# Context attentions: TensorE's transposes issued one by one behind products, with VectorE's and ScalarE's order of a couple of units to match

## Chip, cores and metric

The kernel runs on one core of a Trainium2 chip. The metric is the device time of one execution in microseconds; before the change the median of three runs is 2290.49 us (2285.55 to 2293.77). The time reported for a run is taken around the whole program, and the profile's span lies inside it.

## What is computed

The reference is a stack of four layers on x of shape (8, 64, 256) or, flattened, 512 rows of 256. Each layer adds a cross attention to a context of 1601 keys, a self attention and a feed-forward part, all in float32. Three of the four cross attentions (layer 0's second one, layer 2's, layer 3's) have 16 heads and go through the function that the change touches. Cut to what matters, for layer 2:

```python
scores = jnp.einsum('bhnd,bhmd->bhnm', qh, kh) * scale      # 8 batches, 16 heads, 64 queries, 1601 keys
attn = jax.nn.softmax(scores, axis=-1)
out = jnp.einsum('bhnm,bhmd->bhnd', attn, vh)
```

The kernel does not project the context to keys and values. It takes each head's query through the key weights first, so that the scores are a product of a 128-wide query with the raw 128-wide context, and it takes the weighted sum of the raw context through the value weights afterwards, in another function (`late_values`).

## The kernel before, in words

`cross_attention` (L830) is called three times, at L1860 and L2079 (the latter function twice). A **unit** is two heads of one batch: 2 x 64 = 128 query rows on 128 partitions. There are 64 units (8 batches, 8 units each). Two units make a **couple**, 32 couples in an attention. A step of the engines' loops is 16 units, the first step is written out ahead of the loop.

A float32 operand is kept as two parts of type float32r, a high and a low one, and each product is made of three TensorE products into the same PSUM columns (`three_passes`, L635 to L639): high x high (L637), high x low (L638), low x high (L639).

For each unit v this is done:

- **Scores** (`scores`, L915): four column groups of 290, 512, 512 and 288 keys, three products each, so 12 products, into PSUM banks 0 to 3. The first two groups (802 columns) are the first half, with the semaphore `scores_half`, the others (799) the second, with `scores_ready`.
- **Maximum** (`maximum`, L1079): VectorE takes the maximum of each half (L1082, L1084) and makes the negative scaled maximum `ntop` of both (L1087).
- **Exponents** (`exponents`, L1019): ScalarE writes the exponentials of each half to `probs` (two buffers, called slots: slot 0 is named `normed` in the profile and holds the couple's first unit, slot 1 is named `probs` and holds the second); a small read instruction behind each half fetches the row sums.
- **Transposes** (`turn`, L933): the 1601 probabilities are 13 chunks of 128 keys (the last one has 65). TensorE transposes each chunk (L937) into one of PSUM banks 4, 5 and 7. The chunks form four groups, 4 + 4 + 4 + 1, one bank for a group at a time (`turned_bank`), so a group's first transpose waits until VectorE has emptied that bank (`low_kept`).
- **High and low part** of the transposed probabilities: ScalarE copies a group as high part `pTh` (`keep`, L1031, L1037), then VectorE writes the rest as low part `pTl` (`low`, L1090, L1095), which frees the bank and lets the value products begin.
- **Values** (`values`, L956): both units of a couple at once: 13 chunks, three products of 256 columns each, 39 products, all into PSUM bank 6. VectorE then writes the result back to `q` (`store`, L1100, L1106 or L1108).

The order on each engine is written out by hand. TensorE's order for a couple starting with unit v (`body`, L971) is: transposes of group 0 of the previous couple's second unit; scores(v); transposes of groups 1 and 2 of that second unit; value products of group 0 of the previous couple; transpose of group 3; value products of group 1; scores(v+1); transposes of groups 0 and 1 of unit v; value products of group 2; transposes of group 2; value products of group 3; transpose of group 3 of unit v. So there are five runs of transposes, of 4, 8, 1, 8 and 4, with the last 1 ahead of the next couple's 4. ScalarE's order (L1042): copies of groups 0, 1 and 2 of the previous second unit, both halves of the exponents of v, copy of group 3, in two couples of four a copy of the next batch's keys as high part (`high`, L1014), copies of groups 0 and 1 of v, both halves of the exponents of v+1, copies of groups 2 and 3. VectorE's order (L1110): low part 0 of the previous second unit, maximum of v, low parts 1, 2 and 3, maximum of v+1, low parts 0 and 1 of v, store, low parts 2 and 3 of v. GpSimd (L874) splits the queries of the couple after next and the next keys into parts, and the sync engine (L861) fetches the keys of the next batches; the change touches neither.

These lines of waits matter for the order:

```python
pe.wait_ge(low_kept, 4 * (2 * c + 1) + g + 1)   # in values: low part g of the couple's second unit
act.wait_ge(value_ready if g == 3 else value_part, c if g == 3 else 3 * (c - 1) + g + 1)   # in keep, first unit
```

The first lets a group's value products begin only when VectorE has written that group's low part for the couple's second unit. The second lets a copy of the first unit overwrite `pTh` only when the previous couple's value products of that group are done.

## Time and profile before

| | before |
|---|---|
| median of three runs | 2290.49 us (2285.55 to 2293.77) |
| the profiled execution | 2297.82 us, span 2296.0 us |
| mean granted TensorE clock | 0.93 |
| TensorE products busy | 2042.5 us, 89% |
| TensorE weight loads busy | 1749.3 us, 76% |
| VectorE busy | 1379.2 us, 60% |
| ScalarE busy | 1124.4 us, 49% |
| GpSimd busy | 512.6 us, 22% |
| DMA, mean over the span | 63 GB/s |

The three attentions lie at about 203 to 597, 1107 to 1497 and 1714 to 2107 us of the span. The profile names lines of the kernel and the tiles by the program's names: `ps<-cTh,qh` is a score product, `ps<-pTh,ch` a value product, `ps<-ident,normed` and `ps<-ident,probs` transposes of slots 0 and 1. PE is TensorE's products, PEld its weight loads, which are records of their own; DVE is VectorE, ACT is ScalarE. In a timeline each row gives the start, the duration, the engine, line and operation, shapes and a count of merged instructions. A product's duration contains its way through the array, so products that follow one another overlap in the records: what one costs is read from one start to the next.

### The profile page before, as it was taken

What the parts mean: (1) busy time and instruction counts of PE and PEld (TensorE: products, weight loads), DVE (VectorE), ACT (ScalarE), POOL (GpSimd) and SP (SyncE); (2) the same over time, 40 slices, a digit from 0 to 9 for tenths busy, and PEclk for the clock granted to TensorE, in tenths of its full rate; (3) what the DMA queues carried; (4) which work ended last, traced back from release to release, by engine and by line L of the source; (5) the groups of instructions that cost most, each with busy time, mean ns of one, the idle gap of its engine ahead of it and who ended that gap; (6) DMA issues with size and microseconds to landing.
All of it is one profiled execution on the core that took longest, in us unless ns stands there. A gap on an engine that the chain in (4) does not pass through costs nothing. (4 is left out here: it accounts for less than half of the span.)

```text
span 2296.0 us, 41893 instructions
## 1 busy us (share of the span) xinstructions
PE 2042.5 (89%) x14948; PEld 1749.3 (76%) x14948; DVE 1379.2 (60%) x2704; ACT 1124.4 (49%) x2256; POOL 512.6 (22%) x412
## 2 busy tenths in 40 slices
PE   4776999999886998489899999987979999999898
PEld 1654999999655885277699999956859999997577
DVE  6463777777445443831677777724447777776366
ACT  2243666666423432321566666613436666664254
POOL 2323222221011330200322222002332222220034
PEclk9687999999987998789999999977999999999799
DMA  5153010010041213432100100001221001000022
GB/s 211 25 233 128 31 45 31 29 44 0 26 156 57 79 53 136 188 139 83 45 30 31 45 29 29 0 13 66 78 83 45 31 30 44 29 15 0 19 78 76
DMA packets 32314, 144.01 MB, mean 63 GB/s; under 512 B 3632, under 2 KB 9136, under 8 KB 28848
## 3 DMA queue, kind: packets, MB, share of 16 engines
q1 hardware_dynamic: 32176, 142.23, 17.2%
q8 instruction: 80, 1.31, 0.2%
q14 instruction: 58, 0.48, 0.1%
HBM read 125.59 MB, written 13.90 MB: 61 GB/s over the span
## 5 line engine op out<-in xcount | busy, mean ns | idle before, releaser
L1037 ACT ACTIVATE pTh<-ps 128x512 fp32r<-128x512 f32 (+1 forms) x768 | 353.9, 519 | 382.5 <-PE ps L937 380.4
L1095 DVE TENSOR_TENSOR pTl<-ps,pTh 128x512 fp32r<-128x512 f32 (+1 forms) x768 | 415.7, 582 | 129.0 <-ACT pTh L1037 128.8
L637 PE MATMUL ps<-pTh,ch 128*128 128x256 f32 (+1 forms) x1248 | 383.5, 307 | 2.3 <-DVE pTl L1095 2.2
L638 PE MATMUL ps<-pTl,ch 128*128 128x256 f32 (+1 forms) x1248 | 348.4, 279 | 0.0
L639 PE MATMUL ps<-pTh,cl 128*128 128x256 f32 (+1 forms) x1248 | 348.0, 279 | 0.0
L637 PE MATMUL ps<-cTh,qh 128*128 128x512 f32 (+2 forms) x768 | 276.9, 361 | 15.2 <-POOL ql L891 8.0
L639 PE MATMUL ps<-cTh,ql 128*128 128x512 f32 (+2 forms) x768 | 269.6, 351 | 0.0
L638 PE MATMUL ps<-cTl,qh 128*128 128x512 f32 (+2 forms) x768 | 268.8, 350 | 0.0
L1082 DVE TENSOR_REDUCE top<-ps 128x1 f32<-128x802 f32 x192 | 189.2, 986 | 110.7 <-PE ps L639 110.7
L637 PEld LDWEIGHTS ps<-pTh,ch 128*128 128x128 f32 (+1 forms) x1248 | 235.1, 188 | 15.8 <-DVE pTl L1095 12.1
L638 PEld LDWEIGHTS ps<-pTl,ch 128*128 128x128 f32 (+1 forms) x1248 | 235.7, 189 | 0.0
L639 PEld LDWEIGHTS ps<-pTh,cl 128*128 128x128 f32 (+1 forms) x1248 | 234.5, 188 | 0.0
L1084 DVE TENSOR_REDUCE top<-ps 128x1 f32<-128x799 f32 x192 | 188.7, 983 | 14.8 <-PE ps L639 4.6
L1026 ACT ACTIVATE normed<-ps,ntop 128x802 f32<-128x802 f32 x192 | 176.9, 927 | 32.6 <-DVE ntop L1087 30.5
L937 PE MATMUL ps<-ident,probs 128*128 128x128 f32 (+1 forms) x1248 | 182.9, 272 | 3.5 <-DVE pTl L1095 2.4
L937 PE MATMUL ps<-ident,normed 128*128 128x128 f32 (+1 forms) x1248 | 183.4, 273 | 1.7 <-DVE pTl L1095 1.7
L1026 ACT ACTIVATE probs<-ps,ntop 128x802 f32<-128x802 f32 x192 | 177.0, 938 | 0.0
L637 PEld LDWEIGHTS ps<-cTh,qh 128*128 128x128 f32 x768 | 146.7, 191 | 36.0 <-POOL ql L891 10.5
L638 PEld LDWEIGHTS ps<-cTl,qh 128*128 128x128 f32 x768 | 147.7, 192 | 17.4
L639 PEld LDWEIGHTS ps<-cTh,ql 128*128 128x128 f32 x768 | 147.0, 191 | 16.9
L937 PEld LDWEIGHTS ps<-ident,probs 128*128 128x128 f32 (+1 forms) x1248 | 146.9, 140 | 5.5 <-ACT probs L1026 3.1
L937 PEld LDWEIGHTS ps<-ident,normed 128*128 128x128 f32 (+1 forms) x1248 | 147.0, 141 | 2.4 <-DVE pTl L1095 2.4
(351 smaller groups left out, 3585.9 us busy)
## 6 DMA issues: line engine op xcount, KB each, us to landing
w<-l1f_w_in SPq DMA_DIRECT2D x16, 1024.0 KB, 8.0
raw<-ctxT_in SPq DMA_DIRECT2D x16, 801.0 KB, 4.3
raw<-ctx_in SPq DMA_DIRECT2D x14, 832.0 KB, 4.4
wg<-l0f_guide_in SPq DMA_DIRECT2D x10, 704.0 KB, 5.1
z<-ctx_in SPq DMA_DIRECT2D x8, 832.0 KB, 12.9
z<-z SPq DMA_DIRECT2D x8, 832.0 KB, 10.6
keys<-ctx_in SPq DMA_DIRECT2D x8, 832.0 KB, 11.2
zT<-zT SPq DMA_DIRECT2D x8, 801.0 KB, 14.0
```

What stands on the lines that cost most here:

```text
L637: pe.matmul(out, high, moving_high, start=start, stop=False)
L638: pe.matmul(out, high, moving_low, start=False, stop=False)
L639: return pe.matmul(out, low, moving_high, start=False, stop=stop)
L937: last = pe.transpose(ps[0:w, turned_bank[slot][g], k * P:(k + 1) * P], probs[slot][:, chunk * P:chunk * P + w], ident[:])
L1026: nc.scalar.activation(probs[slot][:, cols], flat[:, cols], ACT.Exp, bias=ntop[:, slot:slot + 1], scale=scale, accum_out=sums[:, bass.ds(2 ...
L1037: nc.scalar.activation(pTh[0:w, PARTS[g][0]:PARTS[g][0] + n, slot, :], ps[0:w, turned_bank[slot][g], 0:n * P].rearrange("p (k r) -> p k r" ...
L1082: dve.tensor_reduce(top[:, slot, 0:1], flat[:, half_cols[0]], AX.X, ALU.max).then_inc(top_step, 1)
L1084: dve.tensor_reduce(top[:, slot, 1:2], flat[:, half_cols[1]], AX.X, ALU.max)\
L1095: dve.tensor_tensor(pTl[0:w, at, slot, :], ps[0:w, turned_bank[slot][g], 0:n * P].rearrange("p (k r) -> p k r", r=P), pTh[0:w, at, slot, : ...
```

## The change

Each transpose is issued by itself behind one product. The functions `scores` and `values` get a parameter `beside`, a function that is called behind each of their products with its number; `turn` issues one transpose. In a couple, the products of scores(v) are numbered 0 to 11, and one transpose of the previous second unit follows each of the products 1 to 4 (group 0) and 8 to 11 (group 1). The value products are numbered 0 to 38: behind 0, 2, 4 and 6 stand group 2's transposes, behind 8 the one of group 3. The value products of chunks 0 to 4 (15 of them) come next, then scores(v+1) without transposes, and then chunks 5 to 12, with the transposes of unit v behind products 15 to 18 (group 0), 19 to 22 (group 1), 25, 27, 29 and 31 (group 2) and 36 (group 3). The wait for `probs_half` ahead of scores(v) stays inside `scores` alone.

On ScalarE the copy of group 2 of the previous second unit moves from ahead of unit v's exponents to behind them, and the second half of unit v+1's exponents moves from ahead of the copies of groups 2 and 3 to behind them. On VectorE the first half's maximum of unit v moves ahead of low part 0 of the previous second unit.

The number of products, transposes, copies and maxima stays the same. The diff, cut to its core:

```diff
 
     @block.tensor
     def _(pe):
-        def scores(u, step, first):
+        def scores(u, step, first, beside):
...
+            k, at = (u // 2) % 2, slice((u % 2) * P, (u % 2) * P + P)
             for n in range(4):
                 if n in (0, 2) and not (first and u == 0):
                     pe.wait_ge(probs_ready if n else probs_half, v)
-                last = three_passes(pe, flat[:, score_cols[n]], qh[:, k, at:at + P],
-                                    ql[:, k, at:at + P], cTh[:, i, score_cols[n]],
-                                    cTl[:, i, score_cols[n]], True, True)
+                cols = score_cols[n]
+                pe.matmul(flat[:, cols], qh[:, k, at], cTh[:, i, cols], start=True, stop=False)
+                beside(3 * n)
+                pe.matmul(flat[:, cols], qh[:, k, at], cTl[:, i, cols], start=False, stop=False)
+                beside(3 * n + 1)
+                last = pe.matmul(flat[:, cols], ql[:, k, at], cTh[:, i, cols], start=False, stop=True)
                 if n == 1:
                     last.then_inc(scores_half, 1)
-            last.then_inc(scores_ready, 1)
...
+                if n == 3:
+                    last.then_inc(scores_ready, 1)
+                beside(3 * n + 2)
+
+        def turn(g, k, v, slot, first=False):
+
+            if k == 0 and slot:
+                pe.wait_ge(low_kept, 4 * v + (-2, -1, 0, 1)[g])
+            if k == 0 and not slot and g != 2 and (g == 3 or not first):
+                pe.wait_ge(low_kept, 4 * v + (-1, 0, None, 1)[g])
+            chunk = PARTS[g][k]
+            w = keys_in(chunk)
+            last = pe.transpose(ps[0:w, turned_bank[slot][g], k * P:(k + 1) * P],
+                                probs[slot][:, chunk * P:chunk * P + w], ident[:])
+            if chunk == PARTS[g][-1]:
+                last.then_inc(turned_ready, 1)
+
...
-            pe.wait_ge(low_kept, 4 * (2 * c + 1) + g + 1)
-            for chunk in PARTS[g]:
-                w = keys_in(chunk)
-                moving = [t[0:w, chunk].rearrange("p u r -> p (u r)") for t in (pTh, pTl)]
-                at = slice(chunk * CD, chunk * CD + CD)
-                last = three_passes(pe, value_psum, ch[0:w, i, at], cl[0:w, i, at],
-                                    moving[0], moving[1], chunk == 0, chunk == KCH - 1)
-            last.then_inc(value_ready if g == 3 else value_part, 1)
+            if chunk % 4 == 0:
+                pe.wait_ge(low_kept, 4 * (2 * c + 1) + g + 1)
+            w = keys_in(chunk)
+            th, tl = (t[0:w, chunk].rearrange("p u r -> p (u r)") for t in (pTh, pTl))
+            at = slice(chunk * CD, chunk * CD + CD)
+            pe.matmul(value_psum, ch[0:w, i, at], th, start=chunk == 0, stop=False)
+            if beside is not None:
+                beside(3 * chunk)
+            pe.matmul(value_psum, ch[0:w, i, at], tl, start=False, stop=False)
+            if beside is not None:
+                beside(3 * chunk + 1)
+            last = pe.matmul(value_psum, cl[0:w, i, at], th, start=False, stop=chunk == KCH - 1)
+            if chunk == PARTS[g][-1]:
+                last.then_inc(value_ready if g == 3 else value_part, 1)
+            if beside is not None:
+                beside(3 * chunk + 2)
+
+        def alone(n):
+            pass
...
                 if first and u == 0:
-                    scores(u, step, first)
-                    scores(u + 1, step, first)
+                    scores(u, step, first, alone)
+                    scores(u + 1, step, first, alone)
                     for g in range(4):
-                        turn_first(g, v, True)
+                        for k in range(len(PARTS[g])):
+                            turn(g, k, v, 0, True)
                     continue
-                pe.wait_ge(probs_half, v)
-                turn_second(0, v - 1)
-                scores(u, step, first)
-                turn_second(1, v - 1)
-                turn_second(2, v - 1)
-                values(0, c - 1, i, first and u == 2, new_batch)
-                turn_second(3, v - 1)
-                values(1, c - 1, i)
-                scores(u + 1, step, first)
-                turn_first(0, v)
-                turn_first(1, v)
-                values(2, c - 1, i)
-                turn_first(2, v)
-                values(3, c - 1, i)
-                turn_first(3, v)
+
+                def second_with_scores(n):
+                    if 1 <= n < 5:
+                        turn(0, n - 1, v - 1, 1)
+                    elif n >= 8:
+                        turn(1, n - 8, v - 1, 1)
+
+                def second_with_values(n):
+                    if n < 8 and n % 2 == 0:
+                        turn(2, n // 2, v - 1, 1)
+                    elif n == 8:
+                        turn(3, 0, v - 1, 1)
+
+                def first_with_values(n):
+                    if 15 <= n < 19:
+                        turn(0, n - 15, v, 0)
+                    elif 19 <= n < 23:
+                        turn(1, n - 19, v, 0)
+                    elif 25 <= n < 33 and n % 2:
+                        turn(2, (n - 25) // 2, v, 0)
+                    elif n == 36:
+                        turn(3, 0, v, 0)
+
+                scores(u, step, first, second_with_scores)
+                values(0, c - 1, i, second_with_values, first and u == 2, new_batch)
+                for chunk in range(1, 4):
+                    values(chunk, c - 1, i, second_with_values)
...
-        values(0, c, 1)
-        values(1, c, 1)
-        values(2, c, 1)
-        values(3, c, 1)
+            for k in range(len(PARTS[g])):
+                turn(g, k, last, 1)
+        for chunk in range(KCH):
+            values(chunk, c, 1)
 
     @block.scalar
     def _(act):
@@ -1048,12 +1070,11 @@
                 before = not (first and u == 0)
                 if before:
                     keep(0, v - 1, 1)
-                if before:
                     keep(1, v - 1, 1)
-                    keep(2, v - 1, 1)
                 exponents(v, 0, first and u < 2, 0)
                 exponents(v, 0, first and u < 2, 1)
                 if before:
+                    keep(2, v - 1, 1)
                     keep(3, v - 1, 1)
                 if at == 0 and not (final and i):
                     high(n, cTh[:, 1 - i])
@@ -1062,9 +1083,9 @@
                 keep(0, v, 0, c if before else None)
                 keep(1, v, 0, c if before else None)
                 exponents(v + 1, 1, first and u < 2, 0)
-                exponents(v + 1, 1, first and u < 2, 1)
                 keep(2, v, 0, c if before else None)
                 keep(3, v, 0, c if before else None)
+                exponents(v + 1, 1, first and u < 2, 1)
 
         body(0, True)
         with act.Fori(1, STEPS - 1) as step:
@@ -1076,10 +1097,13 @@
 
     @block.vector
     def _(dve):
-        def maximum(v, slot):
+        def maximum_of_half(v, slot):
 
             dve.wait_ge(scores_half, v + 1)
             dve.tensor_reduce(top[:, slot, 0:1], flat[:, half_cols[0]], AX.X, ALU.max).then_inc(top_step, 1)
+
+        def maximum(v, slot):
+
             dve.wait_ge(scores_ready, v + 1)
             dve.tensor_reduce(top[:, slot, 1:2], flat[:, half_cols[1]], AX.X, ALU.max)\
                 .then_inc(top_step, 1)
@@ -1113,6 +1137,7 @@
                 v = step * UNITS + u
                 c = step * COUPLES + u // 2
                 before = not (first and u == 0)
+                maximum_of_half(v, 0)
                 if before:
                     low(0, v - 1, 1)
                 maximum(v, 0)
@@ -1120,6 +1145,7 @@
                     low(1, v - 1, 1)
                     low(2, v - 1, 1)
                     low(3, v - 1, 1)
+                maximum_of_half(v + 1, 1)
                 maximum(v + 1, 1)
                 low(0, v, 0)
                 low(1, v, 0)
```

## Rows read from the trace of the kernel before

**Rows 1.** Windows, all engines, inside an attention: busy us, instructions, clock, DMA share, GB/s.
```profile
core 0: us, PE busy (x) PEld busy (x) DVE busy (x) ACT busy (x) POOL busy (x), PEclk, DMA share, GB/s
300.00:350.00 50.00, 50.00 (x370) 47.07 (x369) 36.80 (x64) 33.24 (x71) 11.21 (x10) 1.00 0.11 35
```

**Rows 2.** TensorE's timeline: start, duration; first products of couples 1 and 31, second attention.
```profile
1118.02 0.38 PE L637 MATMUL ps<-cTh,qh 128*128 128x290 f32 x1
...
1478.54 0.38 PE L637 MATMUL ps<-cTh,qh 128*128 128x290 f32 x1
```

**Rows 3.** TensorE's timeline inside one couple of the first attention.
```profile
302.07 0.39 PE L639 MATMUL ps<-cTh,ql 128*128 128x512 f32 x1
302.30 0.30 PE L637 MATMUL ps<-cTh,qh 128*128 128x288 f32 x1
...
302.56 0.30 PE L639 MATMUL ps<-cTh,ql 128*128 128x288 f32 x1
302.70 1.03 PE L937 MATMUL ps<-ident,probs 128*128 128x128 f32 x8
...
303.70 0.28 PE L638 MATMUL ps<-pTl,ch 128*128 128x256 f32 x1
...
304.98 0.27 PE L937 MATMUL ps<-ident,probs 128*65 128x128 f32 x1
...
305.34 0.28 PE L638 MATMUL ps<-pTl,ch 128*128 128x256 f32 x1
...
307.50 0.40 PE L639 MATMUL ps<-cTh,ql 128*128 128x512 f32 x1
```

**Rows 4.** TensorE's weight loads (PEld) in the same stretch, timeline.
```profile
302.07 0.19 PEld L637 LDWEIGHTS ps<-cTh,qh 128*128 128x128 f32 x1
302.30 0.19 PEld L638 LDWEIGHTS ps<-cTl,qh 128*128 128x128 f32 x1
...
303.46 0.19 PEld L637 LDWEIGHTS ps<-pTh,ch 128*128 128x128 f32 x1
303.57 0.19 PEld L638 LDWEIGHTS ps<-pTl,ch 128*128 128x128 f32 x1
...
305.11 0.19 PEld L637 LDWEIGHTS ps<-pTh,ch 128*128 128x128 f32 x1
```

**Rows 5.** VectorE's timeline beside that couple.
```profile
302.34 0.98 DVE L1082 TENSOR_REDUCE top<-ps 128x1 f32<-128x802 f32 x1
303.24 0.97 DVE L1084 TENSOR_REDUCE top<-ps 128x1 f32<-128x799 f32 x1
304.25 0.21 DVE L1087 TENSOR_SCALAR ntop<-top 128x1 f32<-128x1 f32 x1
304.38 1.28 DVE L1095 TENSOR_TENSOR pTl<-ps,pTh 128x512 fp32r<-128x512 f32 x2
...
307.93 0.99 DVE L1082 TENSOR_REDUCE top<-ps 128x1 f32<-128x802 f32 x1 [0.94 <-PE ps L639]
```

**Rows 6.** Groups by line and shape, 240 to 560 us: count, busy us, mean ns.
```profile
L1095 DVE TENSOR_TENSOR pTl<-ps,pTh 128x512 fp32r<-128x512 f32 x160 | 104.8, 683 | 8.6 <-ACT pTh L1037 8.4
```

**Rows 7.** ScalarE's timeline beside that couple.
```profile
303.33 1.09 ACT L1037 ACTIVATE pTh<-ps 128x512 fp32r<-128x512 f32 x2 [1.80 <-PE ps L937]
304.59 0.93 ACT L1026 ACTIVATE normed<-ps,ntop 128x802 f32<-128x802 f32 x1 [0.17 <-DVE ntop L1087]
305.42 0.19 ACT L1026 ACTIVATION_READ_ACCUMULATOR normed<-ps,ntop  x1
...
306.41 0.26 ACT L1037 ACTIVATE pTh<-ps 65x128 fp32r<-65x128 f32 x1
306.57 1.54 ACT L1017 ACTIVATE cTh<-raw 128x1602 fp32r<-128x1602 f32 x1
```

**Rows 8.** TensorE's timeline at the end of the second attention.
```profile
1490.04 0.27 PE L937 MATMUL ps<-ident,normed 128*65 128x128 f32 x1
1490.55 0.66 PE L937 MATMUL ps<-ident,probs 128*128 128x128 f32 x4 [0.24 <-ACT probs L1026]
```

More of the change, by code:

```diff
@@ L921, in scores @@
                                 pe.wait_ge(staged, step * COUPLES + u // 2 + 1)
-                            k, at = (u // 2) % 2, (u % 2) * P
+                            k, at = (u // 2) % 2, slice((u % 2) * P, (u % 2) * P + P)
                             for n in range(4):
@@ L933, in turn @@
-                        def turn(g, v, slot):
-                            for k, chunk in enumerate(PARTS[g]):
-                                w = keys_in(chunk)
-                                last = pe.transpose(ps[0:w, turned_bank[slot][g], k * P:(k + 1) * P],
-                                                    probs[slot][:, chunk * P:chunk * P + w], ident[:])
-                            last.then_inc(turned_ready, 1)
-                        def turn_first(g, v, early=False):
-                            if g == 0 and not early:
-                                pe.wait_ge(low_kept, 4 * v - 1)
-                            if g == 1 and not early:
-                                pe.wait_ge(low_kept, 4 * v)
-                            if g == 3:
-                                pe.wait_ge(low_kept, 4 * v + 1)
-                            turn(g, v, 0)
@@ L951, in turn_second @@
-                        def turn_second(g, v):
-                            pe.wait_ge(low_kept, 4 * v + (-2, -1, 0, 1)[g])
-                            turn(g, v, 1)
-                        def values(g, c, i, early=False, new_batch=None):
-                            if g == 0 and not early:
+                                if n == 3:
[12 more added lines that the diff above has]
+                                last.then_inc(turned_ready, 1)
@@ L959, in values @@
+                        def values(chunk, c, i, beside=None, early=False, new_batch=None):
+                            g = chunk // 4
+                            if chunk == 0 and not early:
                                 pe.wait_ge(value_kept, c)
@@ new lines, in body @@
+                                scores(u, step, first, second_with_scores)
+                                values(0, c - 1, i, second_with_values, first and u == 2, new_batch)
+                                for chunk in range(1, 4):
+                                    values(chunk, c - 1, i, second_with_values)
+                                values(4, c - 1, i)
+                                scores(u + 1, step, first, alone)
+                                for chunk in range(5, KCH):
+                                    values(chunk, c - 1, i, first_with_values)
```

2 lines of the change are left out of this document (removed).

## Prediction

> **What bounds the kernel now.** I read the page first (TensorE is the busiest engine), then windows of 50 us, then TensorE's timeline of one couple, then VectorE's and ScalarE's beside it. Inside an attention TensorE is busy 50.00 us out of 50 at clock 1.00, its level of 2.4 GHz [rows 1]; VectorE has 36.8 and ScalarE 33.2. The page's chain of waits begins behind the last attention and says nothing of this stage, so the measure is TensorE's own period. The first products of couples 1 and 31 of one attention start at 1118.02 and 1478.54 [rows 2]: 360.52/30 = **12.017 us a couple**. An attention has 31 couples behind its first, so there are 93 periods, 1118 us of the span's 2296.
>
> **Is the period full?** The starts in [rows 3] price each kind. A score product of 512 columns takes 0.233 us (302.07 to 302.30), one of 288 or 290 takes 0.134 (302.30 to 302.70 is three), a value product 0.1165 (303.70 to 304.98 is eleven), a transpose in a run (1.03 - 0.27)/7 = 0.109. A couple has 12, 12, 39 and 26 of them: 2.80 + 1.61 + 4.54 + 2.83 = 11.78. A change from transposes to products costs a little: 302.70 to 303.70 is 1.00 for eight transposes (0.872) and a value product (0.117), some 0.01 over; there are five such changes, 0.04. What is left, 12.02 - 11.82 = **0.20 us**, is one wait, at chunk 4's first value product behind the single 65-wide transpose: its load starts only at 305.11 [rows 4], when VectorE's low part of group 1 (started 304.38, 0.68 long [rows 5, 6], so done at 305.06) is there, and 304.98 to 305.34 is 0.36 where 0.23 would do.
>
> **What a transpose costs alone.** The load for the product of 302.30 starts at 302.07, with the product ahead of it, and the next one only at 302.30, although the load port has been free for some 0.12 us; behind the run the loads of two value products stand 0.11 apart (303.46, 303.57) [rows 4], and the second of them starts 0.24 behind the last transpose. Loads thus go one ahead and no further. Whatever follows a transpose, another one or a product, waits 0.109 for its own load. A single transpose hides its own load behind the product ahead, which each product is long enough for, but bares the load of the product behind it. **Its price stays 0.109**; only the edges grow, from 5 to 26. I take 0.008 for an edge (below the 0.01 above, in which rounding lies), so a single transpose takes 0.117, and 21 more edges are 0.17 a couple. Bounds: from below 0.109, the run's price; from above 0.24, the one single transpose of [rows 3] (304.98 to 305.34 less a product). That row holds the wait just named, so I stay by the run's price.
>
> By the Trainium skill, page "TensorE: Matmul & The Clock Gate", section "Step-by-step: what each phase is for", a 64-deep reorder window pulls weight loads ahead of matmuls in flight; if that reached past one load, singles would be cheap. The rows above show no second load ahead; by that rule the third rival's time would come out.
>
> **The wait that goes.** Chunk 4's product now stands behind five more transposes and the longer wait below, so low part 1 (over at 5.1 us from the couple's start, by the order below) comes before it is wanted (5.4). The 0.20 goes.
>
> **The wait that comes.** VectorE now takes the first half's maximum ahead of low part 0, for which chunk 0's first value product waits; before, it took it behind. Number the products of scores(u) 0 to 11. From the start of product 5, VectorE's path is 0.43 until the maximum starts (307.50 [rows 3] to 307.93 [rows 5]), 0.90 for the maximum (302.34 to 303.24), 0.68 for the low part, 0.05 to TensorE (305.06 to 305.11), 0.11 for the held load: **2.17**. ScalarE's copy of group 0 is no limit: its last transpose stands behind product 4 and the copy takes 0.60 (1.09 for two that start 0.49 apart [rows 7]), so it is there before the maximum ends. TensorE's own work in this stretch is four products of 0.233, three of 0.134 and four transposes of 0.117: 0.93 + 0.40 + 0.47 = 1.80. So TensorE stands for **0.37 us a couple**. Queued behind low part 0 on VectorE is the second maximum, and for that wait ntop, ScalarE's exponents and then scores(u+1), which overwrites their banks. From chunk 0's first product on: the second maximum started 0.24 before it and runs 1.01 to ntop, which takes 0.21 [rows 5]; 0.13 later, 304.46 to 304.59, starts the exponent, 1.02 with its read [rows 7]; with 0.05 and 0.11 again that is 2.29, and scores(u+1) is due after 15 value products and 5 transposes, 2.33. Hidden, by 0.04; a miss would lengthen the period.
>
> **The period.** 39 value products 4.54, scores(u+1) 2.20, 18 transposes beside value products 2.11, products 0 to 4 of scores(u) 0.87, their four transposes 0.47: 10.19. With 2.17 it is **12.36**, 0.34 more than 12.017; times 93, **+32 us**.
>
> **Moved on ScalarE.** The copy of group 2 of the second unit stands behind both exponents of the first now: done at 7.0 from the couple's start, its low part at 7.7, while the bank is wanted at 8.1. Hidden, by 0.4. The second half of the second unit's exponents stands behind the copies of groups 2 and 3, and group 2's copy waits for chunk 11's last product (over 0.30 before the couple's end: it starts 0.58 before it). From there 0.03 to start, 0.49 and 0.16 for the two copies, 1.02 for the exponent with its read [rows 7], 0.05 and 0.11 make 1.56 into the next couple, where product 6 is due at 1.10 + 0.47 = 1.57. It fits by 0.01; but a miss comes behind product 5, and up to 0.37 of it is taken out of the stall above. Copies of the next keys keep their place; GpSimd's queue and the DMA issues are untouched.
>
> **At an attention's end** nothing covers that chain. Before, 1490.04 to 1490.55 is 0.51 [rows 8]. After, it is 0.27 + 0.03 + 0.16 + 1.02 + 0.05 + 0.11 = 1.64, less the two products now behind that transpose, 0.23: 1.4. So +0.9, three times, **+2.7**; the 0.56 of idle time behind it stays.
>
> **Sum.** 2297.8 (the profiled execution, span 2296.0 and 1.8 around it) + 32 + 2.7 = 2332.5. That execution lies 7.3 above the median shown; against the median, 2290.5, it is **2325**.
>
> **Rivals.**
> 1. *Cheap edges*: the stall comes, but a single transpose costs 0.109. The 22 outside VectorE's path save 22 x 0.008 = 0.18, 16 us: 2309. Against it stands the 0.01 in [rows 3]; for it, that it is one rounding's size.
> 2. *Faster, the stall hidden*: VectorE's path fits. It decides from where low part 0 comes 0.37 earlier (or TensorE's stretch is that much longer) and an edge costs under 0.006. Only the 0.20 goes: 11.82, -18 us, 2272. Half of it lands within no change.
> 3. *Faster, by loads*: two loads ahead. A transpose then costs half of a value product, 0.058 (an estimate from [rows 3], 128 columns against 256): 22 x 0.059 = 1.30 off the period of 12.36, 11.06, -89 us, 2201. Each pair of loads in [rows 4] speaks against it.
> 4. *Dearer singles*, 0.13: 22 x 0.013 = 0.29, +27 us, 2352; at the upper bound of 0.24, 2.7 a couple, past 2550. Nothing but the row of the bound speaks for it.
> That the edit does nothing is no case: the order on all three engines is written out by hand.
>
> **Chances.** Forecast 0.66 (2310 to 2338); cheap edges and still slower 0.11; dearer 0.08; within 0.3%, about what a measurement of this kernel can tell from no change (2283.6 to 2297.4), 0.07; the second rival 0.05, the third 0.03. So slower 0.85, same 0.07, faster 0.08. The range takes the forecast, most of the cheap edges and the near part of the dearer: 2300 to 2342.
>
> **What would show it.** A period of 12.36 between first score products; the clock still 1.00; one wait a couple, 0.3 to 0.4, of a value product's load for VectorE's low part, at chunk 0 and none at chunk 4; the load behind each single transpose starting with it and the product 0.11 behind. It is wrong if the period is under 12.02, if loads start two ahead, or if TensorE waits for the exponents instead.

## The result, and the profile after

The changed kernel takes **2335.12 us** (median of four runs, 2329.28 to 2336.75) beside 2292.13 us of the kernel before (median of four, with one run more than in the table above): ratio **1.0186**, 95% interval 1.0156 to 1.0216. Run again later it came out at 1.0169 (1.0144 to 1.0193). It is slower by some 1.8%, about 43 us; forecast were 34.7 us more and a time of 2325, so the time lies in the range and on the dear side of the forecast.

The page of the changed kernel: span, busy times (us, share, count) and the granted clock in forty slices of the span, in tenths:

```profile
span 2333.1 us, 41800 instructions
...
PE 2062.8 (88%) x14948; PEld 1750.8 (75%) x14948; DVE 1370.4 (59%) x2704; ACT 1155.1 (50%) x2256; POOL 511.6 (22%) x412
...
PEclk9788999999987998689999999978999999999899
```

TensorE has the same 14948 products and keeps its clock (0.93 in the mean), and its weight loads are as busy as before. Its products' busy time is 20 us more, all of it inside the attentions (1185.7 us for 1164.5): a wait of 0.4 us lies for the most part under the records of the products around it, so it counts as busy. First score products of couples 1 and 31 of the second attention, TensorE's timeline of the changed kernel (answers to [rows 2]):

```profile
1131.05 0.38 PE L927 MATMUL ps<-cTh,qh 128*128 128x290 f32 x1 [0.50 <-ACT probs L1048]
...
1501.32 0.30 PE L927 MATMUL ps<-cTh,qh 128*128 128x290 f32 x1
```

(1501.32 - 1131.05)/30 = **12.342 us a couple**; forecast was 12.36, before it was 12.017. (Couple 1 starts behind a wait of 0.50 that belongs to the attention's beginning.) Where this comes from stands in one couple. TensorE's products in it, start and duration, to be set beside [rows 3]:

```profile
1465.61 0.27 PE L946 MATMUL ps<-ident,probs 128*128 128x128 f32 x1
1465.64 0.47 PE L931 MATMUL ps<-cTh,ql 128*128 128x512 f32 x1
1465.96 0.46 PE L927 MATMUL ps<-cTh,qh 128*128 128x512 f32 x1
1466.26 0.40 PE L929 MATMUL ps<-cTl,qh 128*128 128x512 f32 x1
...
1466.72 0.27 PE L946 MATMUL ps<-ident,probs 128*128 128x128 f32 x1
1466.75 0.38 PE L927 MATMUL ps<-cTh,qh 128*128 128x288 f32 x1
...
1467.45 0.28 PE L946 MATMUL ps<-ident,probs 128*128 128x128 f32 x1
1467.80 0.39 PE L962 MATMUL ps<-pTh,ch 128*128 128x256 f32 x1
1468.02 0.27 PE L946 MATMUL ps<-ident,probs 128*128 128x128 f32 x1
...
1469.41 0.27 PE L946 MATMUL ps<-ident,probs 128*65 128x128 f32 x1
...
1469.76 0.28 PE L968 MATMUL ps<-pTh,cl 128*128 128x256 f32 x1
1469.88 0.28 PE L962 MATMUL ps<-pTh,ch 128*128 128x256 f32 x1
```

and its weight loads (PEld), beside [rows 4]; the bracket gives the idle time before a row and who ended it:

```profile
1465.62 0.19 PEld L931 LDWEIGHTS ps<-cTh,ql 128*128 128x128 f32 x1
1465.91 0.19 PEld L927 LDWEIGHTS ps<-cTh,qh 128*128 128x128 f32 x1
...
1466.49 0.14 PEld L946 LDWEIGHTS ps<-ident,probs 128*128 128x128 f32 x1
1466.73 0.19 PEld L927 LDWEIGHTS ps<-cTh,qh 128*128 128x128 f32 x1
1466.86 0.14 PEld L946 LDWEIGHTS ps<-ident,probs 128*128 128x128 f32 x1
...
1467.80 0.19 PEld L962 LDWEIGHTS ps<-pTh,ch 128*128 128x128 f32 x1 [0.31 <-DVE pTl L1119]
...
1469.76 0.19 PEld L962 LDWEIGHTS ps<-pTh,ch 128*128 128x128 f32 x1
```

VectorE, beside [rows 5], and ScalarE, beside [rows 7], around the same stretch:

```profile
1466.15 0.99 DVE L1103 TENSOR_REDUCE top<-ps 128x1 f32<-128x802 f32 x1 [0.21 <-PE ps L931]
1467.06 0.68 DVE L1119 TENSOR_TENSOR pTl<-ps,pTh 128x512 fp32r<-128x512 f32 x1
1467.66 0.98 DVE L1108 TENSOR_REDUCE top<-ps 128x1 f32<-128x799 f32 x1
...
1468.81 0.68 DVE L1119 TENSOR_TENSOR pTl<-ps,pTh 128x512 fp32r<-128x512 f32 x1
```

```profile
1465.67 0.20 ACT L1048 ACTIVATION_READ_ACCUMULATOR probs<-ps,ntop 128x1 f32 x1
1465.92 0.60 ACT L1059 ACTIVATE pTh<-ps 128x512 fp32r<-128x512 f32 x1
```

What is to be seen:

- **A single transpose costs what one in a run costs.** From the transpose at 1468.02 to the one at 1469.41 are four stretches of a transpose and two value products: 1.39/4 = 0.3475, and 0.109 + 2 x 0.1165 is 0.342. A change from product to transpose and back, the two together, costs 0.0055 us. (That is what the prediction calls an edge of a single transpose; the figure lies within the rounding of the rows, but all 654 such stretches of the trace have a median of 0.348, and experiment 3 gives 0.004.)
- **Loads go one ahead.** The transpose's load starts at 1466.49 with the product ahead of it, the load for the product behind it at 1466.73, 0.01 behind the transpose's start at 1466.72, and the next load 0.13 later. A product behind a transpose is recorded as starting 0.03 behind it, but it lasts 0.08 to 0.1 longer and the next one comes after the full 0.109 + its own time.
- **The wait that comes.** Product 5 follows the transpose of 1465.61, so it begins at 1465.72. VectorE's maximum starts at 1466.15 (0.43 later), low part 0 at 1467.06 (0.91), it takes 0.68, and chunk 0's load starts at 1467.80 [idle 0.31, VectorE's pTl], 0.06 later. With 0.11 for the load this path is 2.19 us; forecast were 2.17. The last transpose of the scores started at 1467.45, its follower's load could have started there: 0.35 us held. Mean over the 90 couples between 1 and 31 of the three attentions, start to start against the kinds' own times: **0.39 us**.
- **A small wait that was said to fit by 0.01.** The exponents' second half with its read is over at 1465.87 (1465.67 + 0.20), product 6's load starts at 1465.91 instead of 1465.73, and product 7 follows at 1466.26 instead of 1466.19. As forecast, it comes out of the stall at chunk 0 and not on top.
- **The wait that goes**, at chunk 4 (mean over the 90 couples before, counted in the same way: 0.18 us): chunk 4's first product now stands behind product 11 and no longer behind the 65-wide transpose. Low part 1 is over at 1469.49 (1468.81 + 0.68), chunk 4's load starts at 1469.76 together with product 11, and its product at 1469.88, 0.12 behind product 11, as any two value products stand. Nothing is held.

At the end of the second attention TensorE shows (beside [rows 8]):

```profile
1513.29 0.27 PE L946 MATMUL ps<-ident,normed 128*65 128x128 f32 x1
...
1515.14 1.53 PE L946 MATMUL ps<-ident,probs 128*128 128x128 f32 x12 [1.34 <-ACT probs L1048]
...
1517.32 0.36 PE L962 MATMUL ps<-pTh,ch 128*128 128x256 f32 x1
```

From the transpose to the next one are 1.85 us where forecast were 1.64. ScalarE in that stretch:

```profile
1513.43 0.76 ACT L1059 ACTIVATE pTh<-ps 128x512 fp32r<-128x512 f32 x2 [0.38 <-PE ps L968]
1514.08 0.92 ACT L1048 ACTIVATE probs<-ps,ntop 128x799 f32<-128x799 f32 x1
```

The copies of groups 2 and 3 start at 1513.43, behind chunk 11's last value product, and the exponents 0.65 later.

The two traces also give a sum by stages. From an attention's first score product to the start of its last value product are 394.39, 390.72 and 393.18 us before and 404.67, 404.19 and 403.99 after: 1178.3 and 1212.9, **+34.6 us**. The other 2.5 us of the span's 37.1 lie outside the changed code (last section).

### The profile page after: what moved, and what is told of

Its sections match the earlier page's. It is cut to its first block and busy times, and to the rows that moved or that the text cites. A ratio compares the mean times of both kernels' runs of the same rounds, so it can differ in the third digit from the quotient of the medians.

```text
span 2333.1 us, 41800 instructions
## 1 busy us (share of the span) xinstructions
PE 2062.8 (88%) x14948; PEld 1750.8 (75%) x14948; DVE 1370.4 (59%) x2704; ACT 1155.1 (50%) x2256; POOL 511.6 (22%) x412
## 5 line engine op out<-in xcount | busy, mean ns | idle before, releaser
L1119 DVE TENSOR_TENSOR pTl<-ps,pTh 128x512 fp32r<-128x512 f32 (+1 forms) x768 | 430.8, 583 | 215.5 <-ACT pTh L1059 215.3
L1059 ACT ACTIVATE pTh<-ps 128x512 fp32r<-128x512 f32 (+1 forms) x768 | 373.7, 515 | 341.7 <-PE ps L946 258.5
L962 PE MATMUL ps<-pTh,ch 128*128 128x256 f32 (+1 forms) x1248 | 400.1, 321 | 12.2 <-DVE pTl L1119 4.0
L965 PE MATMUL ps<-pTl,ch 128*128 128x256 f32 (+1 forms) x1248 | 405.1, 325 | 0.0
L968 PE MATMUL ps<-pTh,cl 128*128 128x256 f32 (+1 forms) x1248 | 397.0, 318 | 0.0
L946 PE MATMUL ps<-ident,probs 128*128 128x128 f32 (+1 forms) x1248 | 324.3, 272 | 5.6 <-ACT probs L1048 4.0
L946 PE MATMUL ps<-ident,normed 128*128 128x128 f32 (+1 forms) x1248 | 308.9, 274 | 1.2 <-DVE pTl L1119 1.2
L931 PE MATMUL ps<-cTh,ql 128*128 128x512 f32 (+2 forms) x768 | 292.2, 380 | 0.0
L946 PEld LDWEIGHTS ps<-ident,probs 128*128 128x128 f32 (+1 forms) x1248 | 173.2, 140 | 11.1 <-ACT probs L1048 4.6
L946 PEld LDWEIGHTS ps<-ident,normed 128*128 128x128 f32 (+1 forms) x1248 | 175.1, 141 | 1.9 <-DVE pTl L1119 1.9
## 6 DMA issues: line engine op xcount, KB each, us to landing
keys<-ctx_in SPq DMA_DIRECT2D x8, 832.0 KB, 11.4
```

What stands on the lines that cost most here:

```text
L931: last = pe.matmul(flat[:, cols], ql[:, k, at], cTh[:, i, cols], start=False, stop=True)
L946: last = pe.transpose(ps[0:w, turned_bank[slot][g], k * P:(k + 1) * P], probs[slot][:, chunk * P:chunk * P + w], ident[:])
L962: pe.matmul(value_psum, ch[0:w, i, at], th, start=chunk == 0, stop=False)
L965: pe.matmul(value_psum, ch[0:w, i, at], tl, start=False, stop=False)
L968: last = pe.matmul(value_psum, cl[0:w, i, at], th, start=False, stop=chunk == KCH - 1)
L1059: nc.scalar.activation(pTh[0:w, PARTS[g][0]:PARTS[g][0] + n, slot, :], ps[0:w, turned_bank[slot][g], 0:n * P].rearrange("p (k r) -> p k r" ...
```

## The experiments

Each was timed in three rounds against the kernel before on its own chip; ratios are to that kernel, with 95% intervals. Mean waits are counted over the 90 couples between 1 and 31 of the three attentions, start to start less each kind's own time. "Period" is the distance of the first score products of couples 1 and 31 of the second attention over 30.

### 1. Undo TensorE's part: before's issue order with the new helpers' order

```diff
 before.py
                                 if before:
                                     keep(0, v - 1, 1)
-                                if before:
                                     keep(1, v - 1, 1)
-                                    keep(2, v - 1, 1)
                                 exponents(v, 0, first and u < 2, 0)
                                 exponents(v, 0, first and u < 2, 1)
                                 if before:
+                                    keep(2, v - 1, 1)
                                     keep(3, v - 1, 1)
...
                                 exponents(v + 1, 1, first and u < 2, 0)
-                                exponents(v + 1, 1, first and u < 2, 1)
                                 keep(2, v, 0, c if before else None)
                                 keep(3, v, 0, c if before else None)
+                                exponents(v + 1, 1, first and u < 2, 1)
...
+                                maximum_of_half(v, 0)
                                 if before:
                                     low(0, v - 1, 1)
                                 maximum(v, 0)
...
+                                maximum_of_half(v + 1, 1)
                                 maximum(v + 1, 1)
```

> TensorE's order of before, with ScalarE's and VectorE's new order. Theory (the whole loss hangs on where the transposes stand: low part 0 is needed only behind the scores, and in the order of before its transposes are over ahead of them): the maximum taken first delays low part 0 here too, but the first value product comes 0.9 us later than its transposes allow, so chunk 0 gets at most 0.05 us of waiting; period 12.0 to 12.06, time within 4 us of before, 2288 to 2296. Rival (the helpers' new order costs by itself, whatever TensorE does): the wait at chunk 0 is there, 0.3 us a couple, period 12.3, time 2318 or more.

Measured: 2291.78 us, ratio 0.9988 (0.9973 to 1.0003), the same time. Its weight loads in one couple:

```profile
1469.73 0.19 PEld L637 LDWEIGHTS ps<-cTh,qh 128*128 128x128 f32 x1 [0.17 <-ACT probs L1026]
...
1473.42 0.19 PEld L637 LDWEIGHTS ps<-pTh,ch 128*128 128x128 f32 x1 [0.15 <-DVE pTl L1097]
```

There are two small waits a couple in place of one, for the exponents ahead of product 6 and for low part 1 at chunk 4. The load's idle time before product 6 is mostly covered by the long product ahead: the means are 0.05 and 0.15, together about before's 0.18. Nothing waits at chunk 0. The 90 periods sum to 1083.5 us, as before. So in the couples the helpers' order costs nothing where the transposes of group 0 stand ahead of the scores; **the whole loss of the couples hangs on where TensorE issues its transposes.** The ends are another matter: from the first unit's last transpose to the next transpose are 1.56 us here, 0.52 before, so nearly all of the 1.1 us that each attention's end loses comes with the helpers' order alone. The time does not show these 3 us, since the stage behind the second attention is 9 us shorter here (last section).

### 2. The changed kernel with low part 0 ahead of the maximum

```diff
 after.py
-                                maximum_of_half(v, 0)
                                 if before:
                                     low(0, v - 1, 1)
+                                maximum_of_half(v, 0)
                                 maximum(v, 0)
```

> The changed kernel with VectorE's first half maximum of the first unit back behind low part 0. Theory (a chain on VectorE sets the pace, not the swap alone: whichever goes first, low part 0, both maxima and ntop have to be over before scores(u+1)): low part 0 starts 0.4 to 0.5 us earlier, but both maxima and with them ntop and the exponents come 0.6 us later, so the wait at chunk 0 goes and waits of 0.3 to 0.55 us come at chunk 4 and 0.15 to 0.4 ahead of scores(u+1); period 12.5 to 12.7, time 2350 to 2370. Rival (the swap is the whole cost): the 0.3 us a couple at chunk 0 goes and nothing takes its place; period 12.05, time 2307.

Measured: 2361.13 us, ratio 1.0281 (1.0235 to 1.0328), some 22 us slower than the changed kernel; period (1522.06 - 1142.43)/30 = 12.654, both as expected. Weight loads in one couple, chunk 0's, chunk 3's last and chunk 4's first:

```profile
1487.36 0.19 PEld L962 LDWEIGHTS ps<-pTh,ch 128*128 128x128 f32 x1
...
1489.21 0.19 PEld L968 LDWEIGHTS ps<-pTh,cl 128*128 128x128 f32 x1
1489.86 0.19 PEld L962 LDWEIGHTS ps<-pTh,ch 128*128 128x128 f32 x1 [0.45 <-DVE pTl L1119]
```

Chunk 0's load (1487.36) waits for nothing, but chunk 4's stands for low part 1, idle 0.45. The means are 0 at chunk 0, 0.53 at chunk 4 and 0.15 ahead of scores(u+1): the wait moved and grew. VectorE's chain through both maxima sets the pace here, and the change's own order on VectorE was the better one for this order on TensorE.

### 3. The changed kernel with its transposes in runs at the last place of each group

```diff
 after.py
-                                    if 1 <= n < 5:
-                                        turn(0, n - 1, v - 1, 1)
-                                    elif n >= 8:
-                                        turn(1, n - 8, v - 1, 1)
+                                    if n == 4:
+                                        turns(0, v - 1, 1)
+                                    elif n == 11:
+                                        turns(1, v - 1, 1)
...
-                                    if n < 8 and n % 2 == 0:
-                                        turn(2, n // 2, v - 1, 1)
+                                    if n == 6:
+                                        turns(2, v - 1, 1)
...
-                                    if 15 <= n < 19:
-                                        turn(0, n - 15, v, 0)
-                                    elif 19 <= n < 23:
-                                        turn(1, n - 19, v, 0)
-                                    elif 25 <= n < 33 and n % 2:
-                                        turn(2, (n - 25) // 2, v, 0)
+                                    if n == 18:
+                                        turns(0, v, 0)
+                                    elif n == 22:
+                                        turns(1, v, 0)
+                                    elif n == 31:
+                                        turns(2, v, 0)
```

(`turns` issues the transposes of a group one behind the other.)

> The changed kernel with each group's transposes issued as one run where its last single one stood (behind products 4 and 11 of the scores, 6, 8, 18, 22, 31 and 36 of the values), helpers as in the change. Theory (a transpose costs 0.109 us wherever it stands, an edge 0.005, and the stall at chunk 0 hangs on the place of the last transpose of group 0 and not on singles): 18 edges fewer, of which 3 lie in VectorE's path and gain nothing: 15 x 0.005 = 0.08 us a couple, 7 us; time 2326 to 2330, the wait at chunk 0 still 0.3. Rival (singles are what costs): period back near 12.05, time below 2310. Rival (singles hide loads and are worth something): slower than the changed kernel, above 2338.

Measured: 2321.38 us, ratio 1.0107 (1.0081 to 1.0134). First score products of couples 1 and 31:

```profile
1133.62 0.37 PE L927 MATMUL ps<-cTh,qh 128*128 128x290 f32 x1 [0.55 <-ACT probs L1052]
...
1502.11 0.30 PE L927 MATMUL ps<-cTh,qh 128*128 128x290 f32 x1
```

and chunk 0's load in one couple:

```profile
1480.99 0.19 PEld L962 LDWEIGHTS ps<-pTh,ch 128*128 128x128 f32 x1 [0.32 <-DVE pTl L1123]
```

The period is 12.283, 0.06 under 12.342; over the 90 periods that is 5.0 us, where some 7 were expected. The three attentions sum to 1206.0 us, 6.8 less than the changed kernel's, but 1.6 of that lie in the first couple of the first attention, which ran at a higher granted clock (last section). The time came out below the expected 2326 to 2330, by the ratios some 18 us under the changed kernel. The profiles do not bear that out in full: their spans differ by 11.4 us. The stage between the second and the third attention is 11.7 us shorter (208.6 for 220.2) and the one between the first and the second 4.8 longer (514.3 for 509.4). The periods are the better measure. The wait at chunk 0 is there as in the changed kernel, mean 0.40. So runs or singles decide some 5 us, and the place of group 0's last transpose and the maximum ahead of its low part decide the rest.

### 4. The kernel before, scores(u+1) two chunks earlier

```diff
 before.py
-                                values(1, c - 1, i)
+                                values(1, c - 1, i, half=0)
                                 scores(u + 1, step, first)
                                 turn_first(0, v)
                                 turn_first(1, v)
+                                values(1, c - 1, i, half=1)
...
                                 exponents(v, 0, first and u < 2, 0)
-                                exponents(v, 0, first and u < 2, 1)
                                 if before:
                                     keep(3, v - 1, 1)
+                                exponents(v, 0, first and u < 2, 1)
...
-                                keep(1, v, 0, c if before else None)
                                 exponents(v + 1, 1, first and u < 2, 0)
+                                keep(1, v, 0, c if before else None)
```

(`half=0` issues chunks 4 and 5, `half=1` chunks 6 and 7.)

> The kernel before with scores(u+1) and the transposes of groups 0 and 1 two chunks of value products earlier, and ScalarE to match: copy of group 3 between the first unit's exponents, the second unit's first half exponents ahead of copy 1. Theory (of before's 12.02 us a couple only 0.20 is waiting, chunk 4 for low part 1, and VectorE reaches low part 1 late because its whole round is late; TensorE's own work, 11.82, is the floor): the wait falls under 0.05, period 11.83 to 11.88, time 2274 to 2280. Rival (the wait only moves, to the exponents ahead of scores(u+1) or to a bank): period 12.0 or more, time 2290 or above.

Measured: 2275.97 us, ratio **0.9914** (0.9887 to 0.9941). It is faster than both kernels.

Its first score products of couples 1 and 31:

```profile
1119.26 0.38 PE L637 MATMUL ps<-cTh,qh 128*128 128x290 f32 x1
...
1474.52 0.38 PE L637 MATMUL ps<-cTh,qh 128*128 128x290 f32 x1
```

The period is 355.26/30 = 11.842, with 0.02 us over the sum of the instructions' own times and five edges: the wait at chunk 4 is gone and none took its place. Over the 90 such periods that is 14.5 us, and this much belongs to the edit. The span is 21.7 us shorter than before: the three attentions whole are 12.5 us shorter (1165.8 for 1178.3), since their first couples are 3.4 us longer together and their ends 1.4 shorter. The other 9.2 us lie in stages that the edit does not touch, 7.9 of them between the second and the third attention (208.8 for 216.8; last section).

### 5. The same without ScalarE's part

The edit is that of experiment 4 without the lines in `exponents` and `keep`.

> The kernel that came out at 0.991 of before, with its TensorE order and ScalarE's order of before. Theory (TensorE's order alone moves the wait: scores(u+1) come two chunks earlier, but the exponents behind copies 1 do not): period 11.95 to 12.0, 2 to 6 us under before. Rival (TensorE's order is the whole gain): period 11.84, 20 us under before.

Measured: 2283.2 us, ratio 0.9942 (0.992 to 0.9963), period (1477.13 - 1118.50)/30 = 11.954, as the theory gave it. The time is 14 us under before where 2 to 6 were expected; the 90 periods give 6.1 us of it, the first couples 1.9, and the other 6 lie outside the attentions.

### 6. The changed kernel with half of the first maximum left out

```diff
 after.py
-                            dve.tensor_reduce(top[:, slot, 0:1], flat[:, half_cols[0]], AX.X, ALU.max).then_inc(top_step, 1)
+                            dve.tensor_reduce(top[:, slot, 0:1], flat[:, 0:SPLIT // 2], AX.X, ALU.max).then_inc(top_step, 1)
```

> The changed kernel with the first maximum of each unit taken over 401 of its 802 columns (the other 401 are left out of the maximum). VectorE's path from product 5 to low part 0 gets 0.4 us shorter. Theory (this path makes the wait at chunk 0, and the path through the second maximum, ntop and exponents lies 0.04 us behind it): the wait at chunk 0 goes, and waits of 0.05 to 0.1 at chunk 4 and 0.15 ahead of scores(u+1) come, so of 0.30 only half is won: period 12.18 to 12.24, 10 to 16 us under the changed kernel. Rival A (VectorE's path at chunk 0 is all): period 12.05, 28 us under it. Rival B (the wait at chunk 0 is for ScalarE's copy, or for a bank): period unchanged, 12.35.

Measured: 2316.85 us, ratio 1.0097 (1.007 to 1.0123), by the ratios 0.7% or some 17 us under the changed kernel on the same chip. That is over the expected 10 to 16; the 90 periods account for 9.1 us, and the stage between the second and the third attention, which the edit does not touch, is 8.5 us shorter (211.7 for 220.2). First score products of couples 1 and 31:

```profile
1125.12 0.37 PE L927 MATMUL ps<-cTh,qh 128*128 128x290 f32 x1 [0.36 <-POOL ql L891]
...
1492.25 0.30 PE L927 MATMUL ps<-cTh,qh 128*128 128x290 f32 x1
```

VectorE's shorter maximum and chunk 0's load in one couple:

```profile
1469.66 0.58 DVE L1103 TENSOR_REDUCE top<-ps 128x1 f32<-128x401 f32 x1 [0.22 <-PE ps L931]
```

```profile
1470.95 0.19 PEld L962 LDWEIGHTS ps<-pTh,ch 128*128 128x128 f32 x1
```

Period 12.238, 0.10 under 12.342. The load at chunk 0 no longer waits: it starts with the last transpose of the scores, which also starts at 1470.95; the means are 0 there, 0.10 at chunk 4 and 0.15 ahead of scores(u+1), 0.25 together where it was 0.39. This shows that VectorE's path through the first maximum made the wait at chunk 0, and that the path through the second maximum, ntop and exponents lies right behind it, as the forecast's 0.04 us had it.

### 7. The changed kernel with ScalarE's order of before

```diff
 after.py
                                     keep(1, v - 1, 1)
+                                    keep(2, v - 1, 1)
                                 exponents(v, 0, first and u < 2, 0)
                                 exponents(v, 0, first and u < 2, 1)
                                 if before:
-                                    keep(2, v - 1, 1)
                                     keep(3, v - 1, 1)
...
                                 exponents(v + 1, 1, first and u < 2, 0)
+                                exponents(v + 1, 1, first and u < 2, 1)
                                 keep(2, v, 0, c if before else None)
                                 keep(3, v, 0, c if before else None)
-                                exponents(v + 1, 1, first and u < 2, 1)
```

> The changed kernel with ScalarE's order of before. Theory (with the transposes spread out, their copies come late, and an exponent behind a late copy holds up the next scores): the copies of groups 2 hold the first unit's exponents until group 2's transposes, behind value products 0 to 6, are over; scores(u+1) waits 0.8 to 0.9 us for them, and the second unit's exponents ahead of copies 2 and 3 gain nothing: period 13.1 to 13.3, time 2405 to 2425. Rival (ScalarE has 6 us of idle time in a couple, its order is worth nothing): within 5 us of the changed kernel.

Measured: 2397.96 us, ratio 1.0443 (1.042 to 1.0466). The two loads of a couple that waited, in the timeline of the weight loads:

```profile
1475.18 0.19 PEld L962 LDWEIGHTS ps<-pTh,ch 128*128 128x128 f32 x1 [0.36 <-DVE pTl L1120]
...
1478.32 0.19 PEld L927 LDWEIGHTS ps<-cTh,qh 128*128 128x128 f32 x1 [0.75 <-ACT normed L1048]
```

and ScalarE's timeline between them:

```profile
1476.76 0.60 ACT L1059 ACTIVATE pTh<-ps 128x512 fp32r<-128x512 f32 x1 [1.07 <-PE ps L946]
1477.26 0.93 ACT L1048 ACTIVATE normed<-ps,ntop 128x802 f32<-128x802 f32 x1
```

ScalarE waits 1.07 us for group 2's transposes, which now end behind value product 6, copies them at 1476.76 and only then starts the exponents at 1477.26, though ntop had been there (VectorE's ntop starts at 1476.06 and takes 0.21); scores(u+1) wait for them (idle 0.75; mean 0.81, beside 0.44 at chunk 0). The period is (1550.90 - 1155.81)/30 = 13.17, as expected; the time is 7 us below the expected 2405. So with TensorE's and VectorE's new order in place, ScalarE's new order saves some 62 us in time (2397.96 for 2336.16) and 74 us in the sum of the three attentions (1286.3 for 1212.7): it is a repair of what TensorE's order does to ScalarE's.

### 8. The changed kernel once more

> The changed kernel once more, beside the other three. The two traces put 34.6 us of the difference inside the three attentions and some 2 to 3 us into stages that the change does not touch. Theory (only the attentions differ): ratio to before 1.013 to 1.018, and the sum of the three attentions again 1212 to 1214 us. Rival (the change also costs something outside, as the medians' 43 us would have it): ratio 1.018 or more and the stages between the attentions longer again.

Measured: 2336.16 us beside 2297.57, ratio 1.0169; attentions 404.55 + 404.25 + 403.94 = 1212.7 us. The sum agrees with the first trace to 0.2 us. The stage between the second and third attention took 220.35 us, 220.24 in the first trace and 216.77 before; the one between the first and the second 513.0, beside 509.4 and 509.2. The theory's ratio came, but the rival is not shut out: the interval reaches 1.0193, and the stages between the attentions were longer again. The other kernels with nearly the same TensorE program (experiments 2, 3, 6 and 7) have 208.6 to 211.7 us between the second and the third attention, which speaks against a cost of the change there.

## Why the prediction was right, and where its sizes were off

- **The period.** 12.36 forecast, 12.342 measured in this attention. Over all 90 periods between couples 1 and 31, 1083.5 us before and 1111.4 after: 0.310 a couple, where 0.34 was said. Before's mean is 12.039 and not 12.017, since one couple of the first attention lasted 13.84; the forecast took one attention.
- **A transpose's price stays 0.109, loads go one ahead.** Right. Two loads ahead, the third rival and the reading of the Trainium skill's reorder window (page "TensorE: Matmul & The Clock Gate", section "Step-by-step: what each phase is for") under which singles would be cheap, did not show: every load behind a single transpose starts with that transpose.
- **The edge.** The term that was mis-sized: 0.008 said, some 0.0055 measured. For 22 edges outside VectorE's path this is 0.055 us a couple, 5 us in all. The first rival's world of free edges did not come either; experiment 3, with 15 such edges fewer, is 0.06 us a couple shorter. The second rival's condition on the edge (under 0.006) was met; what it had wrong is the stall. Its 11.82 also left the 21 new edges out.
- **The wait that comes.** Path 2.17 said, 2.19 measured; stall 0.37 said, 0.39 in the mean, and 0.03 ahead of product 6. Its cause is shown from two sides: experiment 6 shortens the path and the wait goes, experiment 1 has the same helpers without the wait.
- **The wait that goes.** Right, at 0.18 instead of 0.20: nothing is left of it at chunk 4.
- **What was said to be hidden by 0.04** (second maximum, ntop, exponents, scores(u+1)) did stay hidden, and came out in experiment 6, where the stall ahead of it was gone.
- **The end of an attention.** 1.64 said, 1.85 measured. The step took the chain from the last transpose and counted one copy, 0.16. The chain that decides begins with chunk 11's last value product, for which ScalarE's copy of group 2 waits, and holds both copies, 0.65 us from 1513.43 to 1514.08, as the couple's own sum had it. From that transpose to the first value product are 2.68 us before (1490.04 to 1492.72) and 4.03 after; less the two products, 1.1 more and not 0.9.
- **The sum.** 34.7 us were forecast inside the attentions and 34.6 came. That the two agree so closely is luck: the period was 0.03 too dear in the forecast (3 us in all), the ends 0.7 us too cheap, and some 2.4 us come at the beginnings, for which the forecast had no term. Nearly all of that is the second attention's first couple, 11.49 us before and 13.40 after, at a granted clock of 0.85 and 0.62 (last section). The other two first couples had the same clock in both kernels (0.75 and 0.63, 0.74 and 0.62) and got 0.3 us shorter each, by the four transposes that now come later. The medians are 43 us apart. Of what is over the 35 the profiles show 2.5 us outside the changed code; the rest no trace shows. The interval of the ratio is 36 to 50 us, and the second measurement gave 39.

## What to carry to other kernels

Where weight loads go one ahead, as in these traces, an issue order that alternates short and long instructions wins nothing: the short one hides its own load behind the long one, and bares the load of the one behind it. What an issue order does decide is when its results reach the helpers; moving a group of transposes from ahead of a long run of products into it puts their copies, and what waits for them, behind other work of that helper. Price such a change by the path from the last result that the helper needs back to the first instruction that waits for it, and look for a gain in the one wait that the period still has: two chunks of an earlier product took it away here.

## What was not expected of the hardware

The stages outside the attentions differed by up to 13 us between kernels that have the same instructions there, and so did, by some 2 us, the first couple of the second attention. The granted TensorE clock is where they part. The rows are the first couple of the second attention and 27 us of the values' epilogue behind that attention, in windows that start 6.2 to 6.4 us after its last value product. The kernel before:

```profile
core 0: us, PE busy (x) PEld busy (x) DVE busy (x) ACT busy (x) POOL busy (x), PEclk, DMA share, GB/s
1106.53:1118.02 11.49, 8.12 (x42) 6.64 (x42) 5.59 (x8) 5.89 (x10) 4.13 (x4) 0.85 0.17 65
...
1503.50:1530.50 27.00, 25.25 (x59) 9.78 (x54) 6.22 (x9) 6.65 (x10) 0.00 (x0) 0.50 0.00 1
```

the changed kernel:

```profile
1117.65:1131.05 13.40, 10.09 (x37) 8.32 (x38) 5.68 (x8) 5.56 (x10) 5.11 (x5) 0.62 0.21 74
...
1528.20:1555.20 27.00, 25.25 (x56) 9.91 (x53) 6.22 (x9) 6.65 (x10) 0.00 (x0) 0.50 0.00 1
```

experiment 1, the epilogue alone:

```profile
1506.70:1533.70 27.00, 24.47 (x109) 15.14 (x104) 10.14 (x22) 7.70 (x14) 0.00 (x0) 1.00 0.00 1
```

In the epilogue the clock stands at 0.50 (1.2 GHz) in the first two and at 1.00 (2.4 GHz) in the third, in the same stage of the program; in the third TensorE got through 109 products where the first two got through 56 to 59. From the end of the second attention to the start of the third are 216.8, 220.2 and 207.7 us. Before the fall, TensorE had been at the full clock in all of them, with the same thin stretch of 6 us in between (3.12, 3.23 and 3.09 us busy). What tips it is not settled by these runs. It moves a time by some 0.5% without any change in the code under study (the kernel before itself took 2292.9 us at a mean granted clock of 0.932 and 2305.5 at 0.924 in one set of runs), which is why the periods between couples 1 and 31 are the better evidence.
